# An expert layer on one core: where TensorE reads its expert numbers, and when the rows of the tiles are listed

## The chip, the core and the metric

The kernel runs on one core of a Trainium2 chip as one program. The metric is the device time of one execution in microseconds (us), as a median of several runs. The core has TensorE (matmuls and transposes; PE in the profile, PEld for its weight loads), VectorE (DVE), ScalarE (ACT), GpSimd (POOL) and SyncE (SP), each with a sequencer that takes its instructions in order and handles register work, waits and branches by itself. A q behind an engine's name in the profile is its sequencer.

## What is computed

Four batches of 512 tokens with 512 features go through an attention-like mixing block and then a mixture of experts. Cut to what matters here:

```
x = x + cross_mix(ctx, layernorm(x))           # adjacency by a top-k threshold, per batch
h = layernorm(x)                               # 2048 tokens
scores = sigmoid(h @ router_w); top 8 of 32 experts a token (by groups)
routed[t] = sum over its 8 experts e of share[t,e] * (silu(h @ w_gate[e]) * (h @ w_up[e])) @ w_down[e]
shared    = (silu(h @ sw_gate) * (h @ sw_up)) @ sw_down
out = x + routed + shared
```

An expert has 512 x 256 gate and up weights and 256 x 512 down weights, in float32. The kernel computes each product in three float16 matmuls (high by high, high by low, low by high part), so every operand is first split into a high and a low half.

## The kernel before

A first block does the four batches' mixing, the router and most of the shared expert. A second block does the end of the last batch (b = 3) and then all tiles of the routed experts. The rows of each expert are packed into tiles of 128 rows; there are 147 tiles of real or padded rows, in order of their experts, some four or five to an expert.

**Front of the second block.** TensorE finishes the gate and up matmuls of the shared expert, then finds out which rows belong to which tile. `list_tiles` gives for each tile its expert number; DVE puts these into `tile_info` in SBUF (L1345). `turn_found` (L349) turns the last table, ACT copies it (`copy_table`, L367), and `list_rows` of TensorE (L1454, eight matmuls at L1460) and of DVE (L1328) make `ids_i`, the row numbers of all tiles, for which POOL's gathers wait (L1177). Four down blocks `s_down(pe, b, i)` (L282, twelve matmuls at L258 each) make the shared expert's result of the four row blocks; DVE adds each to `acc` (`s_add`, L316), and SP stores `acc` when all are added (L1164). In this kernel TensorE's order is: down block 0, `list_rows`, down blocks 1 and 2, transposes of tiles 0 and 1 (`rows_T`), down block 3, gate and up of tile 0.

**The loop over tiles.** Step t on TensorE is, in this order: R, `rows_T` of tile t + 2 (four transposes, L1490), after its gather; G, `gate_up_of` tile t + 1 (twelve matmuls, L258, stage in PSUM banks 0 and 1), after its rows are split into halves by ACT and DVE and its expert's weights converted; H, `hidden_T` of tile t (two transposes, L1481), after DVE has made `hid`; D, `down_of` tile t - 1 (six matmuls, L258), after ACT and DVE have split the transposed `hid`, and after the result of tile t - 3 has left its bank. ACT copies each result to one of four slots of `y` (L1267), and POOL adds it to the output in memory with a scattering DMA (L1199) and gathers the rows of a later tile (L1187). Where a tile is the first of its expert, its scatter waits for the landing of the one before it (L1192); any scatter waits for the landing of the one before that.

**Weights.** SP loads an expert's 1.5 MB into one of two stages. In the step where an expert's first tile stands, ACT (L240, L241) and then DVE (L247, L250) convert the weights of the expert two further on; each engine does this between its split of the rows and its part of the gates. On DVE the order of a step is: split of rows (L1381), conversion (if any), product (L1389, `hid`), split of hidden (L1398, `hT`).

**The reads.** `info_of(engine, what, t)` (L1153) loads an entry of `tile_info` into a register of the engine's sequencer with `value_load` (its instructions stand at L1156: a TENSOR_LOAD, register work and an assertion). TensorE needs the expert number of the tile of G and of the tile of D to address the weights. It reads both at the start of a step, ahead of R:

```
e, before_e = info_of(pe, 0, t + 1), info_of(pe, 0, t - 1)
rows_T(t + 2, s, (i + 4) % XG)
gate_up_of(t + 1, 1 - s, e)
hidden_T(t, s)
down_of(t - 1, 1 - s, before_e)
```

Steps 0 and 1 are written out, steps 2 to 137 are 17 passes of a loop (L1544) with eight steps each, and the steps from 138 on stand each under a condition on `tile_info` (L1547 to L1551), of which eight are taken with these inputs.

Of the kernel before, what the change touches and what calls it, by code (L numbers as in the profile page):

```python
# [58 lines left out]
def xattn_moe_kernel(nc, x, ctx_in, Wq, Wk, gamma_raw, router_w, router_bias, w_gate, w_up, w_down,  # L59
                     sw_gate, sw_up, sw_down, out):  # L60
    B, N, H = x.shape
    D = ctx_in.shape[2]
    E, _, I = w_gate.shape
    SI = sw_gate.shape[1]
    RT = N // P
# [15 lines left out]
    XG = 8  # L81
# [14 lines left out]
    with ExitStack() as stack:  # L96
# [185 lines left out]
        def s_down(pe, b, i):  # L282

            pe.wait_ge(S["s_lo"], SC * (b + 1))
            if i == RT - 1 and b < B - 1:
                pe.wait_ge(S["added"], RT * b + 1)
            pe.wait_ge(S["s_hid"], SC * (b + 1))
            three(bank[DB[b][i]][:, :], lambda a, c: s_hT16[:, a, c, i * P:(i + 1) * P],
                  lambda w, c: dn16[:, c // IC, w, c % IC, :], SC).then_inc(S["s_down"], 1)
# [26 lines left out]
        def s_add(dve, b, i):  # L316
            dve.wait_ge(S["s_down"], RT * b + i + 1)
            a = acc[:, RT * b + i, :]
            nc.vector.scalar_tensor_tensor(a, bank[DB[b][i]][:, :], 1.0 / W_SCALE, a, ALU.mult, ALU.add).then_inc(S["added"], 1)  # L319
# [833 lines left out]
        def info_of(engine, what, t):  # L1153

            at = tile_info[0:1, what, t:t + 1] if isinstance(t, int) else tile_info[0:1, what, bass.ds(t, 1)]
            return engine.value_load(at, min_val=0, max_val=(E - 1, 1, 1, 16 * NT)[what])  # L1156

        with nc.Block() as block:
# [140 lines left out]
            def _(dve):  # L1299
# [28 lines left out]
                def list_rows():  # L1328

                    dve.wait_ge(S["ids_psum"], 1)  # L1330
                    ch.step(v.tensor_copy(ids[:, :], bank[IDS][:, 0:NT]))
                    ch.step(v.tensor_scalar(pad[:, :], ids[:, :], 0.0, trashf[:, 0:1], ALU.is_le, ALU.mult))
                    ch.step(v.scalar_tensor_tensor(ids[:, :], ids[:, :], -1.0, pad[:, :], ALU.add, ALU.add))
                    v.tensor_copy(ids_i[:, :], ids[:, :]).then_inc(S["ids_ready"], 1)
# [10 lines left out]
                def list_tiles():  # L1345

                    dve.wait_ge(S["info_psum"], 1)
                    ch.done(v.tensor_scalar(tile_info[0:1, 0, :], bank[INFO][0:1, 0:NT], -1.0, None, ALU.add))
                    ch.step(v.tensor_copy(in_use[:, :], bank[INFO][0:1, 3 * NT:3 * NT + 1]))
                    ch.done(v.tensor_scalar(tile_info[0:1, 2, :], tile_nof[0:1, :], in_use[0:1, 0:1], None, ALU.is_le))  # L1350
                    ch.step(v.tensor_scalar(in_use[:, :], in_use[:, :], PLAIN - 1.0, None, ALU.max))
                    ch.step(v.tensor_scalar(last_uses[:, :], tile_nof[0:1, YS - 1::-1], in_use[0:1, 0:1], None, ALU.add))
                    ch.step(v.tensor_copy(results[:, :], last_uses[:, :]))
                    ch.step(v.tensor_scalar(results[:, :], results[:, :], 2, 4, ALU.arith_shift_right, ALU.logical_shift_left))
                    ch.step(v.scalar_tensor_tensor(uses[:, :], uses[:, :], -1.0, bank[INFO][0:1, 2 * NT:3 * NT], ALU.add, ALU.add))
                    ch.done(v.tensor_scalar(tile_info[0:1, 3, :], uses[:, :], 16.0, None, ALU.mult))
                    v.tensor_copy(tile_info[0:1, 1, :], bank[INFO][0:1, NT:2 * NT]).then_inc(S["tables_ready"], 1)


                b = B - 1  # L1360
# [9 lines left out]
                mark(dve, b, 3)  # L1370
                round_uses()
                list_tiles()
                s_add(dve, b, 0)
                list_rows()
                convert_low(dve, SH)
                for i in range(1, RT - 1):
                    s_add(dve, b, i)

                def split_rows(t, s):
# [20 lines left out]
                dve.wait_ge(S["tables_ready"], 1)  # L1400
                split_rows(0, 0)
                split_rows(1, 1)
                s_add(dve, b, RT - 1)
                for e in range(1, AHEAD):
                    convert_low(dve, SH + e)
                gates(0, 0, 0, info_of(dve, 0, 0))
# [22 lines left out]
            def _(pe):  # L1429
# [33 lines left out]
                b = B - 1  # L1463
# [6 lines left out]
                list_tiles()  # L1470
                sum_marks(pe, b)
                turn_found(pe, b)
                s_down(pe, b, 0)
                list_rows()
                for i in range(1, RT - 1):
                    s_down(pe, b, i)
                pe.wait_ge(S["tables_ready"], 1)

# [14 lines left out]
                def gate_up_of(t, s, e):  # L1493

                    pe.wait_ge(S["weights_low"], e * (16 * PIECES) + (SH + 1) * (16 * PIECES))
                    pe.wait_ge(S["rows_low"], t + 1)
                    if not (isinstance(t, int) and t < 2):
                        pe.wait_ge(S["tile_hid"], t - 1)
                    w_slot = (e + SH) % WS
                    three(bank[GU[s]][:, :], lambda a, c: xgT[:, s, a, c, :],  # L1500
                          lambda w, c: gu16[:, bass.ds(w_slot, 1), w, c, :].rearrange("p a n -> p (a n)"), KC).then_inc(S["tile_gu"], 1)
# [8 lines left out]
                def down_of(t, s, e):  # L1510

                    w_slot = (e + SH) % WS
                    pe.wait_ge(S["tile_hlo"], t + 1)
                    if not (isinstance(t, int) and t < 2):
                        pe.wait_ge(S["y_ready"], t - 1)
                    three(bank[DN[s]][:, :], lambda a, c: hT16[:, s, a, c * P:(c + 1) * P],
                          lambda w, c: dn16[:, bass.ds(w_slot, 1), w, c, :].rearrange("p a n -> p (a n)"), IC).then_inc(S["tile_down"], 1)
# [2 lines left out]
                rows_T(0, 0, 0)  # L1520
                pe.wait_ge(S["added"], TT - 2)
                rows_T(1, 1, 1)
                s_down(pe, b, RT - 1)
                gate_up_of(0, 0, info_of(pe, 0, 0))
                pe.wait_ge(S["added"], TT)
                for t in range(2):
                    e, before_e = info_of(pe, 0, t + 1), info_of(pe, 0, 0)
                    rows_T(t + 2, t, t + 2)
                    gate_up_of(t + 1, 1 - t, e)
                    hidden_T(t, t)  # L1530
                    if t:
                        down_of(t - 1, 1 - t, before_e)

                def step(t, i):


                    s = i % 2
                    e, before_e = info_of(pe, 0, t + 1), info_of(pe, 0, t - 1)
                    rows_T(t + 2, s, (i + 4) % XG)
                    gate_up_of(t + 1, 1 - s, e)  # L1540
                    hidden_T(t, s)
                    down_of(t - 1, 1 - s, before_e)

                with pe.Fori(2, PLAIN - XG + 1, XG) as t:  # L1544
                    for i in range(XG):
                        step(t + i, i)
                with pe.Fori(PLAIN, LAST_SKIP + 1, SKIP) as t:  # L1547
                    with pe.If(info_of(pe, 2, t) > 0):
                        for i in range(SKIP):
                            with pe.If(info_of(pe, 2, t + i) > 0):  # L1550
                                step(t + i, i)  # L1551


# [25 lines left out]
```

## Time and profile before

| | us |
|---|---|
| runs of the kernel before | 1042.75, 1042.0, 1039.86 |
| their median | 1042.0 |
| the profiled execution | 1044.03 |
| its span in the profile | 1042.3 |
| TensorE busy (matmuls) | 911.7 |
| VectorE busy | 578.9 |
| ScalarE busy | 500.8 |
| GpSimd busy | 434.7 |

The profile page gives for each engine its busy time. A group or timeline row gives the line, the engine, the operation, the tiles written and read, a count, and in brackets the idle time of the engine before it and what ended it. The chain that ended last is followed back from the last instruction; "issue" in it and in the waits is time in which the engine waited for nothing that the profile shows. A matmul's end is modelled, so rows of adjacent groups overlap a little.

### The profile page before, as it was taken

What the parts mean: (1) busy time and instruction counts of PE and PEld (TensorE: products, weight loads), DVE (VectorE), ACT (ScalarE), POOL (GpSimd) and SP (SyncE); (2) the same over time, 40 slices, a digit from 0 to 9 for tenths busy, and PEclk for the clock granted to TensorE, in tenths of its full rate; (3) what the DMA queues carried; (4) which work ended last, traced back from release to release, by engine and by line L of the source; (5) the groups of instructions that cost most, each with busy time, mean ns of one, the idle gap of its engine ahead of it and who ended that gap; (6) DMA issues with size and microseconds to landing.
All of it is one profiled execution on the core that took longest, in us unless ns stands there. A gap on an engine that the chain in (4) does not pass through costs nothing.

```text
span 1042.3 us, 22025 instructions
## 1 busy us (share of the span) xinstructions
PE 911.7 (87%) x4596; PEld 488.9 (47%) x4597; DVE 578.9 (56%) x1321; ACT 500.8 (48%) x994; POOL 434.7 (42%) x348
## 2 busy tenths in 40 slices
PE   4159787897968999999999999999999999999984
PEld 1144354545434555554545555545545555545542
DVE  5958798888884443446353454444455454463321
ACT  4376482852214443446454454544456455463331
POOL 2011011110032565554655554645645565556642
PEclk8569888798988999999999999999999999999998
DMA  5211021111317688778887778778888888776754
GB/s 155 86 51 53 1 83 53 41 44 41 117 59 262 154 171 182 179 169 212 192 188 163 176 173 212 135 204 185 177 211 185 218 185 221 179 175 131 126 104 75
DMA packets 90270, 149.27 MB, mean 143 GB/s; under 512 B 9648, under 2 KB 46768, under 8 KB 90224
## 3 DMA queue, kind: packets, MB, share of 16 engines
q0 software_dynamic: 33120, 80.64, 39.5%
q1 hardware_dynamic: 57104, 68.13, 20.2%
q8 instruction: 14, 0.23, 0.1%
q14 instruction: 32, 0.26, 0.1%
HBM read 101.55 MB, written 47.20 MB: 143 GB/s over the span
## 4 chain that ended last, share of the span: by engine, by line
PE 62%; issue 4%; DVE 3%; DVEq 1%; ACT 1%; ACTq 1%; DMA 1%; POOL 0%; POOLq 0%
PE bank L258 52%; PE bank L1490 6%; PE bank L1481 3%; DVEq L1156 1%; ACT gu L240 1%; DMA xg<-xrows,ids_i 1%; ACTq L1156 0%; DVE mark_p L400 0%; DVE mark_q L407 0%; DVE gu L247 0%; DVE hid L1389 0%; DVE hid L309 0%; POOL xg L1187 0%; DVE dn L250 0%; POOL out_dram L1199 0%
## 5 line engine op out<-in xcount | busy, mean ns | idle before, releaser
L258 PE MATMUL bank<-gu,xgT 128*128 x1764 | 405.0, 379 | 0.0
L1199 POOL DMA_INDIRECT out_dram<-y,ids_i x145 | 236.2, 1629 | 263.1 <-DMA out_dram<-y,ids_i 165.9
L1381 DVE TENSOR_TENSOR xgT<-bank,xgT 128x512 f16<-128x512 f32 x148 | 102.3, 692 | 285.3 <-ACT xgT L1242 278.4
L258 PEld LDWEIGHTS bank<-gu,xgT 128*128 128x128 f16 x1764 | 172.3, 98 | 175.9 <-issue 0.8
L258 PE MATMUL bank<-dn,hT 128*128 x870 | 211.6, 379 | 0.5
L1187 POOL DMA_INDIRECT xg<-xrows,ids_i x153 | 160.2, 1047 | 74.1 <-issue 39.3
L1242 ACT CAST xgT<-bank 128x512 f16<-128x512 f32 x148 | 86.7, 586 | 140.9 <-issue 88.9
L1267 ACT ACTIVATE y<-bank 128x512 f32<-128x512 f32 x145 | 87.1, 600 | 108.1 <-PE bank L258 107.9
L258 PEld LDWEIGHTS bank<-dn,hT 128*128 128x128 f16 x870 | 85.0, 98 | 74.0 <-issue 6.1
L1389 DVE SCALAR_TENSOR_TENSOR hid<-bank,xg,silu 128x256 f32<-128x256 f32 x147 | 70.7, 481 | 84.0 <-ACT silu L1248 83.7
L1248 ACT ACTIVATE silu<-bank 128x256 f32<-128x256 f32 x147 | 55.9, 380 | 124.9 <-PE bank L258 124.7
L1490 PE MATMUL bank<-ident,xg 128*128 128x128 f32 x592 | 90.4, 276 | 28.9 <-issue 24.0
L1490 PEld LDWEIGHTS bank<-ident,xg 128*128 128x128 f32 x592 | 70.9, 141 | 68.0 <-issue 47.7
L258 PE MATMUL bank<-xT,gu 128*128 128x512 f16 x384 | 86.5, 384 | 4.9 <-DVE acc L319 3.0
L314 POOL TENSOR_TENSOR s_hT<-hid,s_hT 128x512 f16<-128x512 f32 x16 | 22.9, 1433 | 161.6 <-ACT s_hT L302 161.6
L247 DVE SCALAR_TENSOR_TENSOR gu<-stage_gu,gu (+1 forms) x64 | 75.5, 1222 | 18.4 <-ACT gu L240 18.2
L240 ACT ACTIVATE gu<-stage_gu (+1 forms) x64 | 64.2, 1053 | 0.0
L258 PEld LDWEIGHTS bank<-xT,gu 128*128 128x128 f16 x384 | 37.8, 99 | 50.8 <-issue 6.2
L1398 DVE TENSOR_TENSOR hT<-bank,hT 128x256 f16<-128x256 f32 x146 | 60.4, 414 | 0.0
L1481 PE MATMUL bank<-ident,hid 128*128 128x128 f32 x292 | 56.5, 275 | 2.3 <-DVE hid L1389 2.2
L720 ACT ACTIVATE junk<-sim,mid 128x512 bf16<-128x512 f32 x70 | 49.7, 713 | 16.5 <-DVE mid L887 15.6
L1481 PEld LDWEIGHTS bank<-ident,hid 128*128 128x128 f32 x292 | 39.5, 141 | 34.4 <-DVE hid L1389 10.9
(217 smaller groups left out, 775.3 us busy)
## 6 DMA issues: line engine op xcount, KB each, us to landing
stage_gu<-in_L_ffn_w_gate_dram SPq DMA_DIRECT2D x32, 512.0 KB
stage_gu<-in_L_ffn_w_up_dram SPq DMA_DIRECT2D x32, 512.0 KB
stage_dn<-in_L_ffn_w_down_dram SPq DMA_DIRECT2D x32, 512.0 KB
x_sb<-in_x_dram SPq DMA_DIRECT2D x4, 1024.0 KB, 6.5
xrows<-adj SPq DMA_DIRECT2D x4, 1024.0 KB, 4.2
out_dram<-acc SPq DMA_DIRECT2D x4, 1024.0 KB, 4.7
xg<-xrows,ids_i POOLq DMA_INDIRECT x153, 4.5
out_dram<-y,ids_i POOLq DMA_INDIRECT x145, 5.1
```

What stands on the lines that cost most here:

```text
L240: nc.scalar.mul(gu_slot(n, 0, piece), stage_gu(n, piece), W_SCALE).then_inc(S["weights_high"], 1)
L247: nc.vector.scalar_tensor_tensor(gu_slot(n, 1, piece), stage_gu(n, piece), W_SCALE, gu_slot(n, 0, piece), ALU.mult, ALU.subtract).then_inc ...
L258: last = nc.tensor.matmul(out_ap, stationary(a, c), moving(w, c), start=(c == 0 and (a, w) == parts[0]), stop=(c == chunks - 1 and (a, w) ...
L1187: g_.indirect_dma_start(xg[:, t % XG, :], None, xrows, bass.IndirectOffsetOnAxis(ap=ids_i[:, t:t + 1], axis=0)).then_inc(S[f"gathered{t % ...
L1199: g_.indirect_dma_start(out, bass.IndirectOffsetOnAxis(ap=ids_i[:, t:t + 1], axis=0), y[:, t % YS, :], None, compute_op=ALU.add).then_inc( ...
L1242: a_.copy(xgT[:, s, 0, :, :], bank[XB[s]][:, :].rearrange("p (k t) -> p k t", k=KC)).then_inc(S["rows_high"], 1)
L1267: a_.activation(y[:, slot, :], bank[DN[s]][:, :], ACT.Identity, scale=1.0 / W_SCALE).then_inc(S["y_ready"], 1)
L1381: v.tensor_tensor(xgT[:, s, 1, :, :], bank[XB[s]][:, :].rearrange("p (k t) -> p k t", k=KC), xgT[:, s, 0, :, :], ALU.subtract).then_inc(S[ ...
L1389: v.scalar_tensor_tensor(hid[:, s, 0:I], bank[GU[s]][:, I:2 * I], share, silu[:, s, 0:I], ALU.mult, ALU.mult).then_inc(S["tile_hid"], 1)
L1398: v.tensor_tensor(hT16[:, s, 1, :], bank[HT[s]][:, 0:I], hT16[:, s, 0, :], ALU.subtract).then_inc(S["tile_hlo"], 1)
L1481: t = nc.tensor.transpose(bank[HT[s]][:, c * P:(c + 1) * P], hid[:, s, c * P:(c + 1) * P], ident[:, :])
L1490: last = nc.tensor.transpose(bank[XB[s]][:, c * P:(c + 1) * P], xg[:, x, c * P:(c + 1) * P], ident[:, :])
```

## The change

It has two parts. In the second block, TensorE and DVE do `list_rows` ahead of down block 0 and its addition; TensorE then runs the four down blocks one after the other and only after them the transposes of tiles 0 and 1, and DVE's fourth addition moves from behind the splits of tiles 0 and 1 to ahead of them. In the loop over tiles TensorE no longer reads both expert numbers ahead of R. It reads the number for D between G and H, and there too the number for the next step's G, which it hands on to that step as a register. At the start of a pass of the loop one number is read ahead of R, and in the last step of a pass none is handed on. In the conditional steps the number for G is read ahead of R, and that for D behind G. Steps 0 and 1 read the number for G behind R and that for D behind G.

```diff
@@ vector engine
                 round_uses()
                 list_tiles()
+                list_rows()
                 s_add(dve, b, 0)
-                list_rows()
                 convert_low(dve, SH)
-                for i in range(1, RT - 1):
+                for i in range(1, RT):
                     s_add(dve, b, i)
...
                 split_rows(0, 0)
                 split_rows(1, 1)
-                s_add(dve, b, RT - 1)
@@ tensor engine
                 turn_found(pe, b)
-                s_down(pe, b, 0)
                 list_rows()
-                for i in range(1, RT - 1):
+                for i in range(RT):
                     s_down(pe, b, i)
...
                 rows_T(1, 1, 1)
-                s_down(pe, b, RT - 1)
                 gate_up_of(0, 0, info_of(pe, 0, 0))
                 pe.wait_ge(S["added"], TT)
                 for t in range(2):
-                    e, before_e = info_of(pe, 0, t + 1), info_of(pe, 0, 0)
                     rows_T(t + 2, t, t + 2)
-                    gate_up_of(t + 1, 1 - t, e)
+                    gate_up_of(t + 1, 1 - t, info_of(pe, 0, t + 1))
+                    e_down = info_of(pe, 0, 0)
                     hidden_T(t, t)
                     if t:
-                        down_of(t - 1, 1 - t, before_e)
+                        down_of(t - 1, 1 - t, e_down)
 
-                def step(t, i):
+                def step(t, i, e, last=True):
                     s = i % 2
-                    e, before_e = info_of(pe, 0, t + 1), info_of(pe, 0, t - 1)
                     rows_T(t + 2, s, (i + 4) % XG)
                     gate_up_of(t + 1, 1 - s, e)
+                    e_down, e_next = info_of(pe, 0, t - 1), None if last else info_of(pe, 0, t + 2)
                     hidden_T(t, s)
-                    down_of(t - 1, 1 - s, before_e)
+                    down_of(t - 1, 1 - s, e_down)
+                    return e_next
 
                 with pe.Fori(2, PLAIN - XG + 1, XG) as t:
+                    e = info_of(pe, 0, t + 1)
                     for i in range(XG):
-                        step(t + i, i)
+                        e = step(t + i, i, e, i == XG - 1)
...
                             with pe.If(info_of(pe, 2, t + i) > 0):
-                                step(t + i, i)
+                                step(t + i, i, info_of(pe, 0, t + i + 1))
```

## Rows read from the trace of the kernel before

**Rows 1.** The page, part 1: busy time, share of the span, instructions.
```profile
PE 911.7 (87%) x4596; PEld 488.9 (47%) x4597; DVE 578.9 (56%) x1321; ACT 500.8 (48%) x994; POOL 434.7 (42%) x348
```

**Rows 2.** Chain that ended last, 520 to 532 us: start, duration, what.
```profile
519.88 1.29 PE bank L258 x6
521.17 0.44 PE bank L1490 x4
521.61 2.59 PE bank L258 x12
524.20 0.22 PE bank L1481 x2
524.42 1.46 PE bank L258 x6
525.88 1.18 issue
```

**Rows 3.** Waits of PE, 340:981, then 981:1029: us, times, longest.
```profile
PE bank L1490 <- issue: 18.7, 25, 1.4
...
PE bank L1490 <- issue: 5.2, 8, 0.7
```

**Rows 4.** Timeline of DVE, 516 to 536 us: start, duration, instruction.
```profile
523.40 0.48 DVE L1389 SCALAR_TENSOR_TENSOR hid<-bank,xg,silu 128x256 f32<-128x256 f32 x1
523.80 0.41 DVE L1398 TENSOR_TENSOR hT<-bank,hT 128x256 f16<-128x256 f32 x1
```

**Rows 5.** Lines L1156, L1544, L1507 in 524.2:528.9; last row whole run.
```profile
L1156 PEldq TENSOR_LOAD <-tile_info x2: 304/358/413, 525.3 to 526.2; - x2
...
L1544 PEldq ALU_OP  x1: 32/32/32, 524.8 to 524.8; - x1
...
L1507 PEldq EVENT_SEMAPHORE  x1: 51/51/51, 528.4 to 528.4; - x1
...
L1156 PEldq TENSOR_LOAD <-tile_info x304: 294/302/946, 316.5 to 1028.9; - x152
```

**Rows 6.** Timeline of PE, 280 to 350 us.
```profile
306.01 0.74 PE L1460 MATMUL bank<-onehot,tab 128*128 128x164 f16 x8
306.59 5.34 PE L258 MATMUL bank<-dn,s_hT 128*128 128x512 f16 x24
312.79 0.63 PE L1490 MATMUL bank<-ident,xg 128*128 128x128 f32 x4 [0.86 <-DVE acc L319]
...
317.20 5.20 PE L258 MATMUL bank<-dn,s_hT 128*128 128x512 f16 x12
322.24 2.75 PE L258 MATMUL bank<-gu,xgT 128*128 x12
```

**Rows 7.** Timelines of ACT (first two rows) and DVE, 278 to 346 us.
```profile
302.04 0.37 ACT L370 CAST tab<-bank 128x256 f16<-128x256 f32 x1 [0.78 <-PE bank L356]
...
326.91 2.01 ACT L240 ACTIVATE gu<-stage_gu  x2
...
307.88 0.25 DVE L1334 CAST ids_i<-ids 128x164 int32<-128x164 f32 x1
...
314.20 0.69 DVE L1381 TENSOR_TENSOR xgT<-bank,xgT 128x512 f16<-128x512 f32 x1 [1.48 <-ACT xgT L1242]
```

**Rows 8.** Stretches: length, PE, PEld, DVE, ACT, POOL busy, clock, DMA share, GB/s.
```profile
312.00:315.00 3.00, 0.63 (x4) 0.42 (x4) 1.42 (x3) 0.58 (x1) 2.26 (x3) 1.00 0.84 255
315.00:318.00 3.00, 1.68 (x6) 1.15 (x7) 0.00 (x0) 0.55 (x2) 2.21 (x3) 0.55 1.05 370
...
321.00:324.00 3.00, 3.00 (x13) 1.27 (x12) 1.56 (x2) 0.00 (x0) 0.00 (x0) 0.81 0.46 181
```

**Rows 9.** POOL's waits, 796:974; timelines of POOL and ACT, 818 to 850.
```profile
POOL out_dram L1199 <- DMA out_dram<-y,ids_i: 56.4, 11, 7.4
...
835.94 1.59 POOL L1199 DMA_INDIRECT out_dram<-y,ids_i  x1 [6.91 <-DMA out_dram<-y,ids_i]
...
843.07 0.60 ACT L1267 ACTIVATE y<-bank 128x512 f32<-128x512 f32 x1 [0.87 <-PE bank L258]
```

## The prediction

> **What bounds the kernel now.** I read the page's engine line first: TensorE is busy 911.7 of 1042.3 us, no other engine over 579 [rows 1]. So the order of time on TensorE comes next: the chain that ended last, in the main loop [rows 2]. A step there is R (four transposes at L1490, 0.44 us), G (twelve gate and up matmuls at L258, 2.59), H (two transposes at L1481, 0.22) and D (six down matmuls at L258, 1.29): 4.54 us with no hole. Then a D of 1.46 is followed by 1.18 us of "issue", time in which the engine waited for nothing that the profile shows. The waits of TensorE tell how often: 18.7 us before R in 25 gaps of up to 1.4 us, and 5.2 us in 8 gaps in the last steps [rows 3].
>
> Its cause shows around that gap. In a step that converts the next expert's weights DVE comes late: hid is ready at 523.88, for which H (524.20) had waited, and hT at 524.21, for which D had waited [rows 4]. D starts at 524.4. TensorE's sequencer was held at these waits, so nothing is queued behind D, and it still has to read two expert numbers. R starts at 527.06 instead of 525.7. The line of the reads shows two register loads in just this stretch, 304 and 413 ns [rows 5]; each has 0.15 us and more of register work around it. The loop's own register work starts at 524.8, so the pair and the branch take the 2.2 us to R; by the durations I count 0.76 a read.
>
> Ahead of the loop the limit is another: after the third down block (end 311.93) TensorE waits for the gathered rows of tiles 0 and 1, runs the fourth block from 317.20 at the low clock (5.20 us), and G of tile 0 starts at 322.24 [rows 6].
>
> **The reads in the main loop.** Removed: two reads between D and R in seven of eight steps, one in the step that ends a pass. Added: the same number behind G, where 2.59 us of matmuls are queued. No other engine waits for these reads. The profile counts the last matmul of D with its modelled tail (1.46 for 1.29 [rows 2]), so each gap is 0.17 longer than listed: 18.7 + 25 x 0.17 = 23.0 us. After a late D the sequencer now goes to R at once. Two reads (1.5 us) outweigh the gaps, so those of ordinary steps close. A pass ends before every eighth R, and three of the 25 gaps fall there, that at 527.06 among them; there one read stays ahead of R. They are 1.1 to 1.4 us as listed, 0.76 of each is saved, and 1.9 us in sum remain. Saved: 21.1 us.
>
> What the reads cost in the new place: on regular steps nothing, G covers them. The thinnest cover is the step after a late D. D's issue takes 0.5 (524.3 to 524.8), R's and G's 1.5 (R at 527.0, H's wait reached at 528.4 [rows 5]), two reads 1.5: H can be handed on 3.6 us after D's release. TensorE needs it 0.1 + 1.29 + 0.44 + 2.59 = 4.4 after. 0.8 us are left. Single loads take up to 946 ns against a median of 302 [rows 5]; two such in one step would cost 0.5 there. I take off 1 us for all 25.
>
> The Trainium skill, "DMA: Bandwidth & Descriptors", section "Latency and other measured facts", puts the floor of a register load at about 600 ns. The trace differs: 294 at least. By the page's figure the estimate of 4.0 us of sequencer work in a step (rival 5) would be 4.6, over TensorE's 4.54, and the sum some 8 us smaller.
>
> **The last eight steps** stand each under a condition. Their gaps make 4.54 + 5.2 / 8 + 0.17 = 5.36 us a step [rows 3]. The sequencer reads three numbers a step here and H and D never wait for DVE, so its own work is the limit. The change moves one read and takes none away: the sum stays. I take 0; the bounds are 0 and, if the place alone counts, one read each, 8 x 0.76 = 6 us.
>
> **The rows ahead of the down blocks.** The table copy ends at 302.41, so TensorE can list at 302.5 instead of 306.01. At the low clock its 0.74 us become about 1.3. DVE finished the list at 308.13, 1.38 after the listing's end at 306.75 [rows 6, 7]: now at 305.2, 2.9 us earlier, and the eight gathers with it. On DVE the list passes the first addition, which waits for its block in any case; the fourth addition now stands ahead of the first split. TensorE waits 0.5 us for the table at the half clock, worth 0.25 of full-rate work, so the third block ends at 312.2 instead of 311.93. The fourth follows at once at the full clock, 2.67 us (half of 5.34 for two [rows 6]): 314.8. R(0) and R(1) follow, since tile 1's rows, there before 317.20, are there before 314.4 now. G(0) needs DVE's low half of tile 0, which ended at 314.89, 2.1 us after R(0)'s start at 312.79 [rows 6, 7]; DVE's fourth addition fits in between. G(0) starts at 317.0 instead of 322.24: 5.2 us. The first R of the loop has one read fewer ahead of it: 0.8. Front: 6.0 us. The store of the last batch and the first scatter move along; TensorE waits for neither. What is late next: the third expert's load, which starts when its stage is free, as before. The DMA engines were still at 0.46 in 321 to 324 [rows 8], and the conversion moves from 326.91 [rows 7] to 321.7: at worst this gives back 1.5 us.
>
> **What comes late instead.** The scatters are one chain: the first of each expert waits for the landing before it. From 797 to 974 us POOL waits 56.4 us in 11 waits for landings, up to 7.4 [rows 9], so it runs behind. One that had waited 6.91 starts at 835.94, its result made ten us before. With a landing of 4.7 us its slot of y is free at 840.6, and ACT writes that slot at 843.07 [rows 9]: 2.4 us to spare. TensorE saves some 9 gaps of 1.1 us in this stretch and POOL none; ACT can be about 2 us late before TensorE feels it. Walking the chain tile by tile with the old landings leaves 0 to 2 us of stall. I take 1.
>
> **Sum.** 21.1 - 1 + 0 + 6.0 - 1 = 25 us. The profiled execution took 1044.0 (span 1042.3): 1019 for one like it. It lies 2.0 above the median of 1042.0, so the median becomes 1017.
>
> **Rivals.**
> 1. *The clock stays low in front.* The granted clock was 1.00 in 312 to 315 while TensorE was busy 0.63 of 3 us, and fell to a mean of 0.55 in 315 to 318 [rows 8]. In the new order TensorE idles 1.3 us ahead of G(0), with only transposes before it, and the wait at 302 may put off the rise near 305. Price: twelve matmuls took 5.20 us low and 2.75 high [rows 6], so 2.5; a rise 3 us later costs half of that time, 1.5. Time: 1019 to 1021. The Trainium skill, "TensorE: Matmul & The Clock Gate", section "Part 4: PE-mode transpose", says that transposes do not count as activity for the clock; by it R(0) and R(1) would not hold it up. All the work in 312 to 315 was such transposes, so the trace agrees so far.
> 2. *The scatter chain is the bound in the second half.* For it: the 56.4 us. Against it: landings get no slower by themselves. If denser traffic lengthens them, the nine gaps of that stretch give back about 6 us more: 1023.
> 3. *The last eight steps gain too*: 1011.
> 4. *The gap is not the reads*, but the loop's other register work: only the front gains, 1036. Against it: the two loads inside the gap [rows 5].
> 5. *Slower: TensorE's sequencer becomes the bound.* Its work in a step, estimated from the last steps, is 5.36 less one read with its branch (0.86) and less 0.5 for a long load: 4.0 of 4.54 us. If loads behind a full queue of matmuls took their longest form (946 for 302 ns), a step would need 4.0 + 1.3 = 5.3, and 0.76 x 136 steps = 103 us are lost: 1120. It decides from 0.2 us of excess a step (25 us in 136), that is from loads of 0.67 us on the mean. Against it: the median of 304 loads is 302 ns, and in regular steps they fall beside matmuls already.
>
> **How the numbers follow.** Chances: forecast 0.57, rival 1 0.14, rival 2 0.13, rival 3 0.07, rival 4 0.05, rival 5 0.04. Range 1009 to 1026: from rival 3 less 2 us for gaps too small for the list, to rival 2 with the 3 us of rival 1 on top. About 0.3% (3 us) is what a measurement of this kernel can tell from no change. Faster 0.94, within it 0.02, slower 0.04.
>
> **What would show it.** The issue group before R falls from 18.7 to under 4 us and stands at ends of passes; no group appears before H. The sequencer's loads lie beside G. A regular step stays 4.54, the last eight 5.4. G(0) starts near 317, the fourth down block takes 2.7 us. Rival 1 is a G(0) of 5 us; rival 2 is ACT's L1267 waiting for a scatter and TensorE idle after 800 us; rival 4 leaves the 25 gaps; rival 5 is H waiting for issue in every step.

## The result and the profile after

The kernel after takes 1017.7 us (median of 1016.4, 1016.6, 1018.9 and 1019.9) against 1042.4 for the kernel before (four runs beside it): a ratio of 0.977, interval 0.974 to 0.980, or 24.7 us. The forecast was 1017. The profiled execution took 1018.87, with a span of 1017.1.

Page of the kernel after: part 1 and the first row of part 4 (shares of the chain that ended last).

```profile
PE 903.5 (89%) x4596; PEld 489.1 (48%) x4597; DVE 578.3 (57%) x1321; ACT 500.4 (49%) x994; POOL 442.4 (43%) x348
...
PE 48%; issue 7%; DMA 7%; POOL 3%; DVE 3%; ACT 1%; DVEq 1%; ACTq 1%; POOLq 1%
```

The same 4596 matmuls, now 89% of the span instead of 87% [rows 1]. They add up to 8.2 us less, in the main because the modelled tail at each closed gap is gone (0.17 each) and so is the slow block of the front (5.20 us for 2.67). In the kernel before the chain that ended last had PE 62%, issue 4% and DMA 1%; now part of it runs through the landings of scatters. In the new file R stands at L1488 (L1490 before) and H at L1479 (L1481 before); G and D stay at L258.

Waits of TensorE in the kernel after, from 327.6 to 962 us (steps 2 to 137, the main loop), then from 962 to 1005 (the last steps); the columns are us in total, times, longest.

```profile
PE bank L1479 <- DVE hid L1389: 3.9, 7, 1.4
PE bank L1488 <- issue: 1.0, 3, 0.4
PE bank L258 <- DVE xgT L1381: 0.6, 1, 0.6
...
PE bank L1488 <- issue: 4.6, 7, 0.9
```

The 18.7 us before R in 25 gaps [rows 3] are 1.0 in 3. In their place stands a group that was small before: H waits for DVE's `hid`, 3.9 us. The last steps look as they did (5.2 us in 8 then).

The timeline of TensorE around the front, after:

```profile
299.91 0.69 PE L356 MATMUL bank<-ident,found 128*128 128x128 f32 x2 [0.69 <-ACT found L364]
301.06 1.27 PE L1459 MATMUL bank<-onehot,tab 128*128 128x164 f16 x8 [0.46 <-ACT tab L370]
302.13 11.23 PE L258 MATMUL bank<-dn,s_hT 128*128 128x512 f16 x48
313.20 1.04 PE L1488 MATMUL bank<-ident,xg 128*128 128x128 f32 x8
315.60 2.76 PE L258 MATMUL bank<-gu,xgT 128*128 x12 [1.36 <-issue]
...
325.70 0.44 PE L1479 MATMUL bank<-ident,hid 128*128 128x128 f32 x2 [1.06 <-DVE hid L1389]
326.17 1.47 PE L258 MATMUL bank<-dn,hT 128*128 x6
327.68 0.63 PE L1488 MATMUL bank<-ident,xg 128*128 128x128 f32 x4
```

Listing, all four down blocks in one piece of 11.23 us, eight transposes, then G(0) at 315.60 instead of 322.24 [rows 6]. The row at 299.91 is work that the change does not touch; in the kernel before it stood at 301.32, so 1.4 us of the span's difference are the chance of one execution (over all the profiles here this row lies between 298.7 and 301.4).

The starts of a few TensorE rows divide the whole difference:

| stretch, by starts on TensorE | before | after | saved |
|---|---|---|---|
| span's start to the transposes of `found` (L356) | 301.32 | 299.91 | 1.4 |
| from there to G(0) | 20.92 | 15.69 | 5.2 |
| G(0) to the loop's first R, R(4) | 12.94 | 12.08 | 0.9 |
| R(4) to the first R after the loop, 136 steps | 651.4 | 634.0 | 17.4 |
| from there to the last R, seven steps | 38.1 | 37.9 | 0.2 |
| last R to the end | 17.5 | 17.5 | 0 |

The rounded rows add up to 25.1 us, the spans differ by 25.2 and the medians by 24.7.

The same loop divided once more. In both kernels the median step takes 4.54 us, so 136 steps take 617.4, and what is above that is lateness: 34.0 us before, 16.6 after. It is sorted here from the starts of all 136 steps, by which of the four pieces starts later than the one before it ends (1.29, 0.44, 2.59 and 0.22 us [rows 2]); by the choice of these lengths a row can shift by 0.2.

| late piece | before | after |
|---|---|---|
| R (TensorE's own reads and branch) | 24.4 | 1.7 |
| G (split rows) | 1.5 | 0.9 |
| H (`hid`) | 3.2 | 7.0 |
| D (`hT`) | 5.1 | 7.1 |

So 22.7 us were saved at R, and 5.8 of them came back at H and D.

### The profile page after: what moved, and what is told of

Same layout as the page of the kernel before. It is cut to its first block, busy times and chain, and to the rows that moved or that the text cites. A ratio compares the mean times of both kernels' runs of the same rounds, so it can differ in the third digit from the quotient of the medians.

```text
span 1017.1 us, 22025 instructions
## 1 busy us (share of the span) xinstructions
PE 903.5 (89%) x4596; PEld 489.1 (48%) x4597; DVE 578.3 (57%) x1321; ACT 500.4 (49%) x994; POOL 442.4 (43%) x348
## 4 chain that ended last, share of the span: by engine, by line
PE 48%; issue 7%; DMA 7%; POOL 3%; DVE 3%; ACT 1%; DVEq 1%; ACTq 1%; POOLq 1%
PE bank L258 40%; DMA out_dram<-y,ids_i 7%; PE bank L1488 5%; PE bank L1479 3%; POOL out_dram L1199 2%; POOL xg L1187 1%; ACT gu L240 1%; DVEq L1156 1%; ACTq L1156 1%; POOLq L1156 1%; DVE mark_p L400 0%; DVE mark_q L407 0%; DVE gu L247 0%; DVE hid L1389 0%; DVE dn L250 0%
## 5 line engine op out<-in xcount | busy, mean ns | idle before, releaser
L258 PE MATMUL bank<-gu,xgT 128*128 x1764 | 404.9, 379 | 1.9 <-issue 1.4
L258 PEld LDWEIGHTS bank<-gu,xgT 128*128 128x128 f16 x1764 | 172.4, 98 | 177.4 <-issue 2.6
L258 PE MATMUL bank<-dn,hT 128*128 x870 | 211.7, 379 | 0.9
L1187 POOL DMA_INDIRECT xg<-xrows,ids_i x153 | 166.0, 1085 | 68.0 <-issue 43.3
L1267 ACT ACTIVATE y<-bank 128x512 f32<-128x512 f32 x145 | 87.2, 601 | 115.3 <-PE bank L258 91.3
L258 PEld LDWEIGHTS bank<-dn,hT 128*128 128x128 f16 x870 | 84.9, 98 | 75.2 <-issue 7.8
L1488 PE MATMUL bank<-ident,xg 128*128 128x128 f32 x592 | 89.0, 273 | 5.6 <-issue 5.6
L314 POOL TENSOR_TENSOR s_hT<-hid,s_hT 128x512 f16<-128x512 f32 x16 | 22.9, 1433 | 161.6 <-ACT s_hT L302 161.6
L258 PE MATMUL bank<-xT,gu 128*128 128x512 f16 x384 | 86.2, 383 | 5.2 <-DVE acc L319 3.1
L1488 PEld LDWEIGHTS bank<-ident,xg 128*128 128x128 f32 x592 | 73.0, 141 | 36.8 <-issue 10.7
L258 PEld LDWEIGHTS bank<-xT,gu 128*128 128x128 f16 x384 | 37.7, 99 | 50.9 <-issue 5.9
L1479 PE MATMUL bank<-ident,hid 128*128 128x128 f32 x292 | 57.1, 277 | 5.4 <-DVE hid L1389 5.0
L1479 PEld LDWEIGHTS bank<-ident,hid 128*128 128x128 f32 x292 | 38.6, 141 | 40.2 <-DVE hid L1389 16.0
```

The source lines that it names most:

```text
L258: last = nc.tensor.matmul(out_ap, stationary(a, c), moving(w, c), start=(c == 0 and (a, w) == parts[0]), stop=(c == chunks - 1 and (a, w) ...
L1187: g_.indirect_dma_start(xg[:, t % XG, :], None, xrows, bass.IndirectOffsetOnAxis(ap=ids_i[:, t:t + 1], axis=0)).then_inc(S[f"gathered{t % ...
L1267: a_.activation(y[:, slot, :], bank[DN[s]][:, :], ACT.Identity, scale=1.0 / W_SCALE).then_inc(S["y_ready"], 1)
L1479: t = nc.tensor.transpose(bank[HT[s]][:, c * P:(c + 1) * P], hid[:, s, c * P:(c + 1) * P], ident[:, :])
L1488: last = nc.tensor.transpose(bank[XB[s]][:, c * P:(c + 1) * P], xg[:, x, c * P:(c + 1) * P], ident[:, :])
```

## The experiments

**Each part alone.** The kernel before with one of the two parts of the change.

```diff
# front_only: the front of the kernel after, and the loop as before
                 def step(t, i):
                     e, before_e = info_of(pe, 0, t + 1), info_of(pe, 0, t - 1)
                     rows_T(t + 2, s, (i + 4) % XG)
# reads_only: the front of the kernel before, and the loop as after
                 def step(t, i, e, last=True):
                     ...
                     e_down, e_next = info_of(pe, 0, t - 1), None if last else info_of(pe, 0, t + 2)
```

> Only the first part of the change: list_rows ahead of the four down blocks, the loop over tiles as before. If the two parts stand apart, G of tile 0 starts about 5.2 us earlier than before relative to the work ahead of it, the fourth down block takes 2.7 us instead of 5.2, the issue group before R stays at about 24 us in 33 gaps, and the median is 1042.4 - 5.2 = 1037. If the front's gain is lost behind the first scatter or a weight load, it is 1040 or more.

> Only the second part: the order of the front as before, the reads behind G. If the gaps before R are the reads, the issue group of the loop falls from 18.7 us to under 4 and the median is 1042.4 - 19.5 = 1023. The whole change measured 1017.7, so the parts would add up. If the front carried more than I think, this one is at 1026 or more.

The front alone: 1038.0 us against 1042.1 for the kernel before beside it, a ratio of 0.9964 (0.9949 to 0.9979), which is 3.8 us (2.2 to 5.3). The reads alone: 1020.3, a ratio of 0.9805 (0.9772 to 0.9839), 20.3 us. Together 24.1, and the whole change 24.7: they add up as far as these intervals can tell. The front gave less than the 5.2 us expected, which lie just inside its interval. The waits of TensorE between 340 and 960 us, first of the front alone, then of the reads alone:

```profile
PE bank L1488 <- issue: 17.8, 26, 1.3
PE bank L1479 <- DVE hid L1389: 0.8, 2, 0.5
```

```profile
PE bank L1481 <- DVE hid L1389: 2.4, 7, 0.6
PE bank L1490 <- issue: 1.0, 3, 0.4
```

The gaps before R go with the reads and not with the front; the loop of the reads alone takes 631.9 us. In the profile of the front alone G(0) comes 15.66 us after the row of `found`, as in the kernel after, so the 5.2 us are there; that execution took 1034.5 us, 3.5 less than the median of its kernel.

**How much a read is worth in its old place.** The kernel before, with D's number alone behind G.

```diff
-                    e, before_e = info_of(pe, 0, t + 1), info_of(pe, 0, t - 1)
+                    e = info_of(pe, 0, t + 1)
                     rows_T(t + 2, s, (i + 4) % XG)
                     gate_up_of(t + 1, 1 - s, e)
+                    before_e = info_of(pe, 0, t - 1)
```

> Before, with only the number for D read behind G; the number for G is still read ahead of R. Theory (a gap is the time of the reads between D and R, 0.76 us each): of 25 gaps of 0.92 us on the mean (0.75 as listed and 0.17 of tail) 0.2 to 0.3 are left on the mean, the listed issue group falls from 18.7 to about 3 to 4 us, and of the gain of the full change in the loop about three quarters are there: 1027 to 1029. Rival (the gap is the loop's other register work, or the place of the read does not matter): 1042. Rival (moving either read is enough, because only the order counts): 1023.

Measured 1021.2 us, a ratio of 0.983 (0.978 to 0.987). I had expected 1027 to 1029, so this is a miss: one read gives nearly all of what two give (0.981 for the reads alone, with overlapping intervals). The waits between 340 and 960 us:

```profile
PE bank L1481 <- DVE hid L1389: 2.1, 6, 0.7
PE bank L1490 <- issue: 1.3, 4, 0.4
```

In the kernel before there were 28 gaps over 0.2 us before R, of 0.2 to 1.6. Each could at most give back itself, and 12 were shorter than the 0.76 us of one read. What stands beyond 0.76 in the 16 others adds up to 5.1 us; 2.9 us are left before R in this kernel. The second read thus had only some 3 to 5 us to give, and I had priced it as if it stood in every gap with its whole length.

**How much room is behind G.** The kernel after, with one or two unused reads more in each step.

```diff
                     e_down, e_next = info_of(pe, 0, t - 1), None if last else info_of(pe, 0, t + 2)
+                    info_of(pe, 0, t)        # extra1
+                    info_of(pe, 0, t)        # extra2 has both
```

> The changed kernel with one more read of an expert number behind G in each step, its value unused. Theory (the sequencer's own work is about 4.0 us of a step's 4.54, and a read adds 0.76): a regular step becomes 4.8 us, sequencer-bound, and the last eight about 6.1: 0.25 x 136 less what is hidden in late steps, plus 6, so 1017.7 + 30 to 40 = 1048 to 1058. Rival (the sequencer has room for another read): steps stay 4.54 and only the last eight grow, 1024.

> The same with two more reads. Theory: a regular step of 5.5 us and the last eight of 6.9, so 1.0 x 136 + 12 more: about 1165. The difference of a regular step between extra1 and extra2 is the price of one read, 0.76 us. Rival (the sequencer has room): under 1060.

One read more: 1034.4 us, a ratio of 0.991 (0.989 to 0.993) to the kernel before, some 17 us over the kernel after. Two more: 1120.2, a single run. The first is 14 us under the least that I expected, the second 45 us under: both are misses. The waits of TensorE in the loop, first with one read more (322 to 975 us), then with two (322 to 1048):

```profile
PE bank L1479 <- issue: 8.2, 18, 1.1
PE bank L1479 <- DVE hid L1389: 2.9, 7, 1.1
```

```profile
PE bank L1479 <- issue: 41.5, 104, 1.8
PE bank L1479 <- DVE hid L1389: 23.4, 16, 1.8
```

And a stretch of the timeline of TensorE with two more:

```profile
504.85 2.75 PE L258 MATMUL bank<-gu,xgT 128*128 x12
507.82 0.41 PE L1479 MATMUL bank<-ident,hid 128*128 128x128 f32 x2 [0.21 <-issue]
508.11 1.47 PE L258 MATMUL bank<-dn,hT 128*128 x6
509.41 0.60 PE L1488 MATMUL bank<-ident,xg 128*128 128x128 f32 x4
509.85 2.75 PE L258 MATMUL bank<-gu,xgT 128*128 x12
512.86 0.41 PE L1479 MATMUL bank<-ident,hid 128*128 128x128 f32 x2 [0.26 <-issue]
```

With three reads behind G the median step is still 4.54 us, and H is late in 37 of 136. With four it is 5.05, from R to R, and H is late in 120 of 136. Now the sequencer's own work is the step: 5.05, less two reads. A read here is a load of 302 ns, a register operation of 151, as a rule another of about 45, an assertion of 18 and the pauses between them: 0.64 to 0.75 us from the start of one read to that of the next. By this estimate the kernel after needs 3.5 to 3.8 of its 4.54. So rival 5 doesn't begin at the change; one read beyond it costs in single steps, and the second in every step.

**What the scatters cost.** The kernel after with eight slots of `y` instead of four. The room in SBUF comes from `xgT`, which is laid over a tile that is no longer used; a control has only that, with four slots.

```diff
-    YS = 4
+    YS = 8                                   # slots8 alone
...
-        xgT = sb("xgT", [P, 2, 2, KC, P], F16)
+        xgT = s_hT16[:, 0, :, :].rearrange("p (s a) (k t) -> p s a k t", s=2, k=KC)
```

> The changed kernel with eight slots of y in place of four (the split rows xgT take the place of the shared expert's hidden halves, which are dead by then). Theory (part of the gain is given back because ACT waits for a scatter to land before it may write a slot: five waits, 11.7 us on ACT, which TensorE feels as about 3 us before H and G after 790 us): no such wait is left, and the median is 1017.7 - 3 = 1014.7. Rival (TensorE would have waited in these steps for the conversion of weights in any case): 1017.7 or up to 1 us less.

> The changed kernel with four slots of y as it has, and only xgT laid over the dead hidden halves as in slots8: the control of that run. Theory: the place of xgT costs nothing, so this is the changed kernel again, 1017.7 (1015 to 1020), with ACT waiting again for scatters in the second half (about 10 us) and TensorE for H or G there (about 3 us). Rival (the place of xgT is what kept slots8 from gaining): 1021 or more, with longer weight loads or splits.

In the kernel after, ACT waits for slots of `y`, which it never did before. Its waits from 340 to 960 us and one such wait, in the timelines of ACT (first three rows), DVE (next three) and TensorE (last):

```profile
ACT y L1267 <- DMA out_dram<-y,ids_i: 11.7, 5, 3.5
...
860.63 0.60 ACT L1267 ACTIVATE y<-bank 128x512 f32<-128x512 f32 x1 [2.47 <-DMA out_dram<-y,ids_i]
862.00 0.58 ACT L1242 CAST xgT<-bank 128x512 f16<-128x512 f32 x1 [0.78 <-PE bank L258]
862.49 2.00 ACT L240 ACTIVATE gu<-stage_gu  x2
...
863.96 2.36 DVE L247 SCALAR_TENSOR_TENSOR gu<-stage_gu,gu  x2 [0.65 <-ACT gu L240]
866.24 1.22 DVE L250 SCALAR_TENSOR_TENSOR dn<-stage_dn,dn  x1
867.37 0.48 DVE L1389 SCALAR_TENSOR_TENSOR hid<-bank,xg,silu 128x256 f32<-128x256 f32 x1
...
867.90 0.44 PE L1479 MATMUL bank<-ident,hid 128*128 128x128 f32 x2 [1.35 <-DVE hid L1389]
```

Here one reads the whole way from a scatter to TensorE. ACT writes `y` at 860.63, 2.47 us late. Behind it on ACT stands the split of the next rows (862.00) and behind that the conversion of an expert's weights (862.49), which pushes DVE's conversion to 863.96, its `hid` to 867.37 and H to 867.90. A late scatter alone is absorbed for the most part: after the longest wait, 3.50 us, no step lost more than 0.75. It hurts more where a conversion follows it.

In the kernel after two steps are late for a scatter: this one, 117, by 1.78 us in all, and 106, by 0.75 (G waits for `xgT`, 1.37 us behind that 3.50 us wait). In the control they are 1.77 and 0.59 late. With eight slots the waits of ACT are gone and the two steps are 0.67 and 0 late, so the scatters cost 1.7 to 1.9 us. Yet the kernel takes 1021.0 us (0.981, 0.978 to 0.984) where 1014.7 was expected, a miss, while the control takes 1016.1 (0.975, 0.972 to 0.978), as expected. The loops are alike, 633.0 us with eight slots and 633.2 in the control. Elsewhere in the loop a gather came late,

```profile
PE bank L1488 <- DMA xg<-xrows,ids_i: 1.3, 1, 1.3
```

and POOL ends the kernel by reading the count of each slot and waiting for it, eight reads instead of four: the stretch behind the last R is 20.2 us instead of 17.4. Another 2.7 us lie in the last seven steps (37.8 against 35.2), which differ as much between profiles with the same code of TensorE (37.9 and 37.6 in two profiles of the kernel after, 35.7 in the reads alone). So by the traces the scatter waits are worth a little under 2 us, but eight slots don't bring them in.

**What the conversions cost.** The kernel after, in which DVE makes the low part of the down weights (1.22 us) behind this step's `hid` and `hT` instead of ahead of them.

```diff
                     split_rows(t + 2, s)
-                    next_weights(fresh, e)                       # gate, up and down
+                    next_weights(fresh, e + (SH + AHEAD))        # gate and up
                     gates(t + 1, 1 - s, (x + 1) % XG, next_e)
                     hidden(t, s)
+                    next_down(fresh, e + (SH + AHEAD))           # down
```

> The changed kernel with one conversion moved on DVE: the low part of the down weights (1.22 us) is made behind hid and hT of its step, not ahead of them. Theory (what is left of the loss, 14 us of H and D waiting in 24 steps, is DVE making hid and hT behind three conversions): hid and hT come 1.2 us earlier there, TensorE waits for neither, and the median is 1017.7 - 10 to 13 = 1005 to 1008. Rival (the moved conversion makes the next split of rows late, and G waits instead, or the extra branch costs DVE's sequencer as much): 1017 or more.

Measured 1013.0 us, a ratio of 0.971 (0.969 to 0.973): the fastest kernel of this study, 4.8 us under the kernel after by the medians and about 6 by the ratios (0.977, and 0.976 in a second set), but only half the gain that I expected. The control with four slots, measured beside it, has 0.975 (0.972 to 0.978), only 4.3 us more. The waits of TensorE in its loop (322 to 956 us; H is L1489 there) and a converting step of DVE:

```profile
PE bank L258 <- DVE xgT L1381: 4.4, 9, 0.9
PE bank L258 <- issue: 3.7, 7, 0.8
PE bank L1489 <- DVE hid L1389: 0.3, 1, 0.3
...
509.15 0.48 DVE L1389 SCALAR_TENSOR_TENSOR hid<-bank,xg,silu 128x256 f32<-128x256 f32 x1
509.54 0.41 DVE L1407 TENSOR_TENSOR hT<-bank,hT 128x256 f16<-128x256 f32 x1
509.87 1.22 DVE L1402 SCALAR_TENSOR_TENSOR dn<-stage_dn,dn  x1
511.62 0.69 DVE L1381 TENSOR_TENSOR xgT<-bank,xgT 128x512 f16<-128x512 f32 x1 [0.54 <-issue]
```

H and D together are late by 1.8 us in the loop instead of 14.1, so 12.3 of the 14.1 go away when the queue ahead of `hid` is 1.22 us shorter. But now the next split of rows stands behind the 1.22 us, and G is late by 12.0 us instead of 0.9. The seven waits of G that are listed as issue belong to it: in each of them DVE's split ended 0.19 to 0.26 us ahead of G, as in those listed under its name. The lateness was moved one piece on, and only 2.8 of 16.6 us went; another 1.0 us is saved ahead of the loop, where in the kernel after H had waited 1.06 us for `hid` (at 325.70).

The next step was to put the down part behind the next step's split, where it would hit neither; and that with eight slots too.

```diff
                     split_rows(t + 2, s)
+                    if late is not None: next_down(*late)        # of the step before
                     next_weights(fresh, n)
                     gates(t + 1, 1 - s, (x + 1) % XG, next_e)
                     hidden(t, s)
+                    if last: next_down(fresh, n)                 # step that ends a pass
```

> As late_down_low, but the low part of the down weights is made one step later, behind that step's split of rows. late_down_low turned the waits before H and D into waits of G for the split of rows (4.4 us listed in 9 places). Theory (DVE's conversion was too much for one step in any order, but fits in two): no H, D or G waits for DVE in converting steps, the loop's loss falls from some 16 us to 5 (three ends of passes at 0.5, scatter waits about 3), and the median is 1005 to 1009. Rival (ACT's three conversions, 3 us, are the longer part and DVE only follows): 1012 or more. Rival (the later release of the stage makes a weight load late): ACT waits for a load, 1013 or more.

> late_down_next with the eight slots of y of slots8. Theory (with TensorE faster the scatters fall further behind, so the slot waits cost more here than in the changed kernel): 3 us less than late_down_next, less the 1.4 us of one late gather that slots8 showed: 1 to 3 us under it. Rival (slot waits are hidden on ACT): the same as late_down_next or 1.5 us over it.

> The changed kernel itself, on the chip of the next two for a fair comparison: 1017.7, within 3 us.

The kernel after, beside them, takes 1018.3 us (0.976, 0.975 to 0.978), as before. The later place takes 1019.9 (0.980, 0.977 to 0.982) and with eight slots 1023.1 (0.980, 0.977 to 0.983): both are misses. Waits of ACT and TensorE with the later place, and of TensorE with eight slots as well (340 to 960 us):

```profile
ACT gu L240 <- DMA stage_dn<-in_L_ffn_w_down_dram: 3.2, 2, 2.0
```

```profile
PE bank L258 <- DVE xgT L1381: 2.9, 5, 0.9
PE bank L1495 <- DVE hid L1389: 2.4, 5, 0.9
```

```profile
PE bank L1504 <- DMA xg<-xrows,ids_i: 6.7, 4, 2.9
```

The stage of the down weights is set free a step later, so the load of a later expert starts later, and where experts follow each other closely ACT now waits for that load. That is the second rival above; it was right in kind, but 3.2 us in two waits are not all of the lateness, and what makes the rest was not separated. Lateness in the loop is 17.0 us, as in the kernel after (16.6), only distributed otherwise: 7.6 at G, 6.4 at H. With eight slots it is 22.9: gathers arrive up to 2.9 us late. POOL takes scatters and gathers in turn. Before the longest of these waits it had stood 6.82 and 6.00 us for landings ahead of two scatters, and issued the gather only 7.0 us ahead of its R (491.62 and 498.62); in the kernel after, the same gather goes out 13.3 us ahead. It also took 6.9 us to land, against 4.7. Why POOL falls further behind with eight slots was not tested and stays open.

## Why the prediction was right, point by point

**The cause of the gaps.** Right. Rival 4 (not the reads) is refuted by the reads alone, 1020 us where it would have left all 25 gaps. The register loads of the kernel after lie behind G, but for one at the start of a pass and those of the last steps, and their durations are those of [rows 5], 302 ns at the median: the price of the loads is the same, and what changed is what runs beside them.

```profile
L1156 PEldq TENSOR_LOAD <-tile_info x303: 295/302/980, 316.7 to 1004.7; - x152
```

**Gaps before R.** Predicted: 23.0 us of gaps, 21.1 saved, 1.9 left at ends of passes. By the starts of the steps 24.4, 22.7 and 1.7; the three that are left are 0.53, 0.49 and 0.48 us. Right, with 1.6 us more saved than I summed.

**Reads behind G.** Predicted: nothing in regular steps, 0.8 us of room after a late D, 1 us for long loads. Right in effect; H waited for issue in no listed wait of the profiled loop. The one so listed in the second profile of the same kernel, 1.1 us, is step 117 again: H starts there 0.05 us behind the end of `hid`. The working of rival 5 was too dark: I estimated 4.0 us of sequencer work from the last steps, and the kernels with more reads give 3.5 to 3.8.

**The front.** Predicted 6.0: 5.2 to G(0), 0.8 to the first R of the loop. Measured 5.2 and 0.9 in the profiled pair; the runs of the front alone give 3.8 (2.2 to 5.3), so that the times bear out the traces only roughly. Each step came as told, the third and fourth blocks at full clock among them. Counted from the row of `found`, the fourth block ends at 13.3 us, where I had 13.5, and G(0) follows that end by 2.4 us, where I had 2.2. The third expert's load gave nothing back that the sum would show.

**The clock (rival 1).** Not seen. Stretches of the kernel after (length, PE, PEld, DVE, ACT, POOL busy, granted clock, DMA share, GB/s):

```profile
303.00:306.00 3.00, 3.00 (x14) 1.37 (x13) 0.99 (x4) 0.00 (x0) 1.72 (x2) 0.91 0.08 16
...
312.00:315.00 3.00, 2.24 (x15) 1.34 (x13) 1.11 (x2) 1.11 (x3) 2.29 (x3) 1.00 1.09 372
315.00:318.00 3.00, 2.40 (x12) 1.19 (x13) 2.85 (x4) 2.81 (x3) 0.55 (x1) 1.00 1.02 400
```

The clock rose within 303 to 306 (mean 0.91; 0.65 in the kernel before, which was 1.4 us later here), so no later than before, and stayed at 1.00 over the transposes and the 1.36 us without work ahead of G(0). In the kernel before, 315 to 318 had 0.55 [rows 8], after 312 to 315 with 0.63 us of work. The Trainium skill, "TensorE: Matmul & The Clock Gate", section "Part 4: PE-mode transpose", says that transposes don't count as activity for the clock. By that rule the time from 313.20 to 315.60 was idle for the clock, and it stayed up all the same; the rule is not refuted by it, since matmuls stood right before and after these 2.4 us. In the kernel before, 5.3 us between two down blocks (311.93 to 317.20) held nothing but eight transposes, and the clock fell; but TensorE was idle for most of that time, so it doesn't tell what transposes alone would do.

**The last steps (rival 3).** Predicted nothing, with a bound of 6 us. Measured 0.2 in the profiled pair. But both profiles with the last steps of the kernel before (it and the front alone) have 38.1 us, and the eight with those of the kernel after lie between 35.2 and 38.6, with a mean of 37.0; with one read moved it is 35.1. So perhaps 1 us was gained here; the pair can't tell it.

**What comes late instead.** This is the term that was mis-sized. I took off 1 us for the scatters and 1 for long loads, 2 in all; lateness at G, H and D rose by 5.2, from 9.8 to 15.0. Of this the scatters are 1.7 to 1.9 (steps 106 and 117, above). The mechanism was the one named: ACT's L1267 waits, five times and 11.7 us in all, and TensorE feels it after 800 us. But I walked the chain of scatters alone, and not what stands behind the late `y` on ACT, in step 117 a conversion. The other 3.4 us are conversions without any scatter, as in step 103, and in the step that answers to [rows 4]. The rows of DVE and TensorE there:

```profile
510.16 1.22 DVE L250 SCALAR_TENSOR_TENSOR dn<-stage_dn,dn  x1
511.30 0.48 DVE L1389 SCALAR_TENSOR_TENSOR hid<-bank,xg,silu 128x256 f32<-128x256 f32 x1
...
511.83 0.44 PE L1479 MATMUL bank<-ident,hid 128*128 128x128 f32 x2 [0.39 <-DVE hid L1389]
```

DVE has 3.58 us of conversion (2.36 and 1.22) in a step of 4.54, and H waits in more steps than before (16 over 0.1 us instead of 7) and for longer. Every one of these waits, in both kernels, stands behind a conversion, and so does every late D. The kernel that moves 1.22 us of it shows the same: 14.1 us become 1.8.

Why the conversions end later than before is another question, and ACT answers most of it. DVE's conversion waits for ACT's, and ACT's stands behind its split of the rows. ACT begins a step with two reads of its own, ahead of that split. Its loads of this step, and the split in the kernel after and in the same step of the kernel before:

```profile
L1156 ACTq TENSOR_LOAD <-tile_info x2: 282/606/931, 504.0 to 504.6; - x2
...
505.93 0.58 ACT L1242 CAST xgT<-bank 128x512 f16<-128x512 f32 x1 [1.42 <-issue]
...
518.04 0.58 ACT L1242 CAST xgT<-bank 128x512 f16<-128x512 f32 x1 [0.77 <-issue]
```

One load took 931 ns, where both took about 280 before. The split starts 2.22 us behind R (503.71) instead of 1.57 (516.47), and H is 0.55 us late. In the other converting steps too H is late, within 0.05 us but for one, by what this distance has above 1.67 us; over the 29 conversions of the loop it is 1.90 on the mean, and was 1.61. The 5.8 us more at H and D come from three places: about 1.6 in step 117 (the scatter), 1.8 in five converting steps that stood behind a pause of 0.4 to 1.3 us at R before the change and weren't late at all then, and 2.5 in the 23 others, where no such pause was lost. So the lost pauses account for under a third. In the others long loads on ACT have a large part: 8 of the 29 conversions now have more than 0.2 us of them ahead of the split, and 4 had before. The front alone has 3, the other kernels with moved reads 7 to 11, except for that with four reads behind G, which has 5. Why moving TensorE's reads should lengthen ACT's, no run shows. In the reads alone no scatter holds ACT up in the loop, and H and D are late by 12.6 us all the same (7.1 in the front alone).

**Why the number still fits.** The sum foretold 25.0 us. Without the 1.4 us of chance ahead of the front, the profiled pair gives 23.7: 17.4 in the loop, where 19.1 were due, 6.1 in front, where 6.0 were, and 0.2 in the last steps. The medians give 24.7. In the loop two errors partly cancel: R gave 1.6 us more than summed, and lateness at G, H and D took 5.2 where I had 2. What is left, 1.7 us, is within the spread of single runs (1016.4 to 1019.9), so that the median agrees to a microsecond is partly luck.

## What to carry to other kernels

A gap before an instruction that "waits for nothing" is often the sequencer's own work, but not always (seven such waits of G above were waits for DVE): see what the sequencer does there, and what ended just before. If it reads, move the read behind the longest piece that is already queued, to a place where the sequencer isn't just coming from a wait. The engines behind TensorE have such reads too: one long load ahead of ACT's split reached H as 0.55 us. Count the room from the wait's release, not from the mean of a step: one read more left the median step alone and still cost 17 us, and two more cost 100. And a gap that closes was also slack for the engines behind it: before summing, look which of them came late by a little, and what long job stands in their queue.

## What the runs showed that I had not expected

- The cost of a read on TensorE's sequencer depends nearly all on its place: up to 0.64 to 0.75 us each between D and R, nothing behind G for the first two, about 17 us in the whole for a third (0.12 us a step) and 86 us for a fourth (0.6 a step).
- Single loads of a register take long forms without any visible cause: 302 to 304 ns at the median of every kernel on TensorE, up to 946, 980, 1001 and 1141 ns in four of them.
- Taking a wait off one queue can make another late: with eight slots of `y`, ACT's waits for scatters went from 12.0 us (in the control) to none, and R waited for gathers, 1.3 us in one kernel and 6.7 in the other.
